# A gated two-layer cross-attention model on one core: rope's repeated query block removed, its halves exchanged by 64-partition vector instructions, a head pair's first projection one slot further ahead

## The reference, cut to what matters

```python
# x (8,112,512), ctx (8,375,128); 16 heads, K=128, D_CQ=384, R=64; layer 0's attention:
q_hk  = (layernorm(x) @ Wq.T).reshape(8, 112, 16, 128)
q_big = einsum('bshk,hkq->bshq', q_hk, w_kc_q)             # 384 wide
q_big = q_big*cos + rotate_half(q_big)*sin                 # rotate_half(x) = [-x[192:], x[:192]]
kv_r  = ctx*cos + rotate_half(ctx)*sin
q_r, k_r = q_big @ W_qr, kv_r @ W_kr                       # 64 wide
ctx_c = softmax(q_r @ k_r.T) @ kv_r                        # 112 x 375 scores per head
x = x + tanh(g) * ((ctx_c @ w_kc_kv.T) @ Wo.T)
# then a quantised feed-forward, a second attention (no rope on the query), a second feed-forward
```

## Time and profile before

| | |
|---|---|
| runs | 1081.9, 1082.13, 1083.32 us; median 1082.13 us |
| profiled execution | 1087.78 us, its span 1085.7 us, mean granted clock 0.983 |
| PE busy | 988.6 us, 91% of the span |
| DVE, ACT, POOL busy | 674.6, 530.9, 516.5 us |
| layer 0's attention | the first scores at 69.22 us, one pair of heads every 49.95 us |

### The profile page before, as it was taken

The page is one execution under the profiler, slowest core; times in us unless marked ns, Lnnn a source line. Parts: engine busy times, 40 slices in busy tenths (PEclk is TensorE's granted clock), DMA queues, the critical chain, the costliest instruction groups (busy, mean ns, idle before and its releaser), DMA issues. The chain is left out here.

```text
span 1085.7 us, 19735 instructions
## 1 busy us (share of the span) xinstructions
PE 988.6 (91%) x6228; PEld 575.3 (53%) x6237; DVE 674.6 (62%) x1176; ACT 530.9 (49%) x1238; POOL 516.5 (48%) x651
## 2 busy tenths in 40 slices
PE   0678999999999999899999689999999989999998
PEld 0335555555555555544444357777777754444543
DVE  2768787877878787659767726666666662423012
ACT  1245556565656566600257337777777772105400
POOL 1947666676666667511224326666666660200000
PEclk9999999999999999999999979999999999998999
DMA  8020312212130201055020122210222004104001
GB/s 216 25 81 19 102 48 64 68 43 68 43 92 29 92 19 30 11 198 191 1 69 30 40 68 69 69 34 34 68 68 68 1 1 184 39 1 165 1 29 39
DMA packets 24603, 68.24 MB, mean 63 GB/s; under 512 B 3696, under 2 KB 5872, under 8 KB 22259
## 3 DMA queue, kind: packets, MB, share of 16 engines
q1 hardware_dynamic: 18368, 56.70, 15.7%
q10 hardware_dynamic: 6192, 10.97, 3.8%
HBM read 63.98 MB, written 3.68 MB: 62 GB/s over the span
## 5 line engine op out<-in xcount | busy, mean ns | idle before, releaser
L1077 POOL TENSOR_SCALAR scratch<-scratch,rinv 112x375 f32<-112x375 f32 x256 | 155.4, 621 | 148.5 <-DVE rinv L944 148.5
L819 ACT ACTIVATE scratch<-ps,mxn 112x375 f32<-112x375 f32 x256 | 144.1, 571 | 58.5 <-DVE mxn L939 58.4
L939 DVE TENSOR_REDUCE mxn<-ps 112x2 f32<-112x750 f32 x128 | 119.5, 934 | 41.3 <-PE ps L633 41.3
L1059 POOL TENSOR_TENSOR scratch<-scratch 128x896 f32<-128x896 f32 x64 | 104.4, 1632 | 59.4 <-DVE scratch L963 58.9
L684 PE MATMUL ps<-xnT,scratch 128*128 128x448 f16 x576 | 125.1, 364 | 3.8 <-DVE scratch L1014 2.4
L671 PE MATMUL ps<-scratch,kvn_hi 125*128 125x224 f16 x768 | 119.9, 260 | 4.4 <-DVE scratch L985 2.3
L656 PEld LDWEIGHTS ps<-ident,scratch 112*125 112x125 f32 x768 | 100.0, 188 | 42.4 <-issue 35.3
L1069 POOL TENSOR_TENSOR scratch<-scratch 128x375 f16<-128x375 f32 x128 | 115.3, 901 | 10.9
L656 PE MATMUL ps<-ident,scratch 112*125 112x112 f32 x768 | 106.5, 275 | 10.9 <-DVE scratch L1005 9.1
L829 ACT ACTIVATE scratch<-ps 125x672 f16<-125x672 f32 x128 | 94.2, 736 | 43.5 <-PE ps L656 42.5
L963 DVE TENSOR_TENSOR scratch<-ps,ropeq 128x448 f32<-128x448 f32 x192 | 108.2, 615 | 7.3 <-PE ps L684 6.8
(11 more groups left out here) (161 smaller groups left out, 1485.6 us busy)
## 6 DMA issues: line engine op xcount, KB each, us to landing
scratch<-in_wq SPq DMA_DIRECT2D x16, 512.0 KB, 5.2
scratch<-in_wo SPq DMA_DIRECT2D x16, 512.0 KB, 3.7
wabs<-in_w ACTq DMA_DIRECT2D x32, 256.0 KB, 3.0
scratch<-in_w SPq DMA_DIRECT2D x8, 1024.0 KB, 4.9
scratch<-in_W SPq DMA_DIRECT2D x8, 1024.0 KB, 5.8
scratch<-in_kcq SPq DMA_DIRECT2D x8, 512.0 KB, 5.2
scratch<-in_qr SPq DMA_DIRECT2D x32, 128.0 KB, 3.1
scratch<-in_kcq SPq DMA_DIRECT2D x8, 384.0 KB, 3.2
```

The costliest lines, as they stand in the source:

```text
L819: last = nc.scalar.activation(prob[0:S, s % 2, hh, :], scores_ps[0:S, hh, 0:L], ACT.Exp, bias=mxn[0:S, s % 2, hh:hh + 1], accum_out=rsum[0 ...
L939: nc.vector.tensor_reduce(mxn[0:S, s % 2, :], scores_ps[0:S, :, 0:L], AX_X, ALU.max, negate=True).then_inc(max_done, 1)
L1059: nc.gpsimd.tensor_tensor(roped[:, u % 2, rows], roped[:, u % 2, rows], turned[:, rows], ALU.add).then_inc(rope_add, 1)
L1077: last = nc.gpsimd.tensor_scalar(prob[0:S, s % 2, hh, :], prob[0:S, s % 2, hh, :], rinv[0:S, s % 2, hh:hh + 1], P_SCALE, ALU.mult, ALU.mult)
```

## The change

Block 3 goes. Its table row in `ropeq` is loaded with its halves exchanged, and `rope` makes the rotated product of block 2 with two instructions of 64 partitions: one reads partitions 64 to 127 of PSUM and writes partitions 0 to 63, the other the reverse. `w_kc_q` is split for 384 channels per head, not 512. The blocks come in the order 2, 0, 1, and POOL's two additions count on semaphores of their own. The order on all engines is a new one: B comes early in a slot and A at its end; A 0 of the next pair stands in slot 3 ahead of C 1 (it was in slot 4), A 2 in slot 7 ahead of C 0 (it was in slot 0 of its own pair). SP loads Wq, w_kc_q, W_qr and W_kr one pair further ahead.

```diff
 TENSOR = ([
-    [TURN, SCORES, ("A", 2), ("S", 0), ("K", 2), *ropes(2, 0, 1)],
-    [TURN, SCORES, ("A", 3), ("S", 1), ("K", 3), *ropes(2, 2, 3)],
+    [TURN, SCORES, *ropes(2, 2, 0), ("S", 0), ("K", 2), ("A", 3)],
+    [TURN, SCORES, *ropes(2, 1), ("S", 1), ("K", 3), *ropes(3, 2)],
...
 VECTOR = ([
-    [SCORES, TURN, NORM, ("A", 3), ("S", 1), *ropes(2, 2, 3)],
+    [SCORES, TURN, *ropes(2, 1), NORM, ("S", 1), *ropes(3, 2)],
...
-            act.dma_start(ropeq[:, :, :], tab["ropeq"]).then_inc(s_ropeq, 16)
+            act.dma_start(ropeq[:, 0:5, :], tab["ropeq"][:, 0:5, :]).then_inc(s_ropeq, 16)
+            act.dma_start(ropeq[0:R, 5, :], tab["ropeq"][R:P, 5, :]).then_inc(s_ropeq, 16)
+            act.dma_start(ropeq[R:P, 5, :], tab["ropeq"][0:R, 5, :]).then_inc(s_ropeq, 16)
...
+            mixed = order[at["A", 0]:N_THIS] if layer == 0 else []
...
+                    def iteration(p):
+                        last = isinstance(p, int) and p + 2 >= PAIRS
+                        if is_batch(p) and is_batch(p + 1):
+                            weights(p + 1, "kckv", "wo")
+                        if not last:
+                            weights(p + 2, "wq", "kcq")
+                        if not last:
+                            weights(p + 2, "qr")
...
-                            pe.wait_ge(rope_add, nth(q, 8, 4 * n + 3))
+                            pe.wait_ge(rope_add, nth(q, 4, 2 * n + 1))
+                            pe.wait_ge(last_add, nth(q, 4, 2 * n + 1))
...
-                                       ((roped[:, u % 2, 2], 2),),
-                                       ((turned[:, 2], 5),))[j]:
+                                ((roped[:, u % 2, 2], 2, every, every), (turned[:, 2], 5, high, low),
+                                 (turned[:, 2], 5, low, high)))[j]:
+                            n_rows = rows.stop - rows.start
                             last = nc.vector.tensor_tensor(
-                                dst.rearrange("p (b n) -> p b n", b=B // 2), src,
-                                ropeq[:, t:t + 1, :].to_broadcast([P, B // 2, S]), ALU.mult)
+                                dst[to].rearrange("p (b n) -> p b n", b=B // 2), src[rows],
+                                ropeq[rows, t:t + 1, :].to_broadcast([n_rows, B // 2, S]),
+                                ALU.mult)
```

More of the change, by code:

```diff
@@ L260, in flamingo, with load_pair @@
         s_gate = sem("gates_done")
-        def load_pair(sp, layer, q, free=None):
+        def load_pair(sp, layer, q, free=None, names=()):
             order = ("qr", "kcq", "wq") if layer == 1 or free is not None else ("wq", "kcq", "qr")
-            for n in order + ("kckv", "wo"):
+            for n in names or order + ("kckv", "wo"):
                 src = w[f"{n}{layer}"][ds(q, 1)]
@@ L481, in attention @@
             N_THIS = at["C" if layer == 0 else "Q", 1] + 1
-            this = order[:N_THIS]
+            this = [g for g in order[:N_THIS] if g != ("A", 0)]
+            mixed = order[at["A", 0]:N_THIS] if layer == 0 else []
+            N_AHEAD = N_THIS - len(mixed)
             last_u = max((("U", 0), ("U", 1)), key=lambda g: (g in this, at[g]))
@@ L536, in first, with counts @@
                 return isinstance(p, int) and p < 0
+            def counts(p, g):
+                return 1 + any(x != g and g in mixed and not runs(p, x) for x in mixed)
             kv_behind = {5: (0, 1), 6: (2, 3, 4), 7: (5, 6, 7)}
@@ L616, in free @@
                                            nth_group(q - 1, ("M" if n == "wq" else "W", 0)))
-                        load_pair(sp, layer, q, free)
+                        load_pair(sp, layer, q, free, names)
+                    def iteration(p):
[6 more added lines that the diff above has]
+                            weights(p + 2, "qr")
+                    if layer == 0:
+                        iteration(-1)
+                        with sp.Fori(0, PAIRS - 2) as p:
+                            iteration(p)
+                        iteration(PAIRS - 2)
+                        iteration(PAIRS - 1)
+                    else:
+                        with sp.Fori(1, PAIRS) as q:
+                            weights(q)
                 @block.tensor
@@ L775, in group @@
                                         start=True, stop=True)
-                        last.then_inc(group_done, 1)
+                        last.then_inc(group_done, counts(p, g))
                     def iteration(p, slots=range(B)):
@@ L926, in _ @@
                     act.sem_inc(exp_done, 1)
-                    act.sem_inc(group_high, sum(g in split_order for g in this))
+                    act.sem_inc(group_high, sum(g in split_order for g in order[:N_AHEAD]))
                     iteration(-1)
```

105 lines of the change are left out of this document (56 added, 49 removed).

## The result

The changed kernel takes 1094.91 us (median of 4 runs, 1092.71 to 1096.45) where before takes 1082.02 beside it (4 runs): the ratio is 1.0119, with an interval of [1.0094, 1.0145]. It is slower by 12.9 us. The forecast was 1088, slower, with a range of 1076 to 1093: the direction holds, the size doesn't, and the median lies 1.9 us outside the range.

What follows compares the result with a forecast made beforehand. PE was taken as the bound, its gain nearly all given back as waits for DVE. Seven pairs +2.45, start +5.3, last pair -1.2: +6.5 us, 1087.78 to 1094.3; less 5.65, 1088.6, given as 1088, range 1076 to 1093.

Steps and rivals of the forecast that it cites:

- the places named: PE waits for DVE at A 3, A 1, U 0, A 0, X, R, B 1 2 and U 1: together 4.6 us a pair.
- the price of crossing: DVE instructions of block 2 that change partitions take 0.61 us, not 0.53: 1.0 us a pair on DVE, 0.85 on the path.
- the upper of the two bounds: A crossing DVE instruction can't start under the tail of the one before: 0.64 us; the lower bound was 0.53.
- the forecast's 0.85 a pair for the holds alone: Crossing price on the path: A 3 and A 1 0.17 each, U 0 0.26, B 1 2 / U 1 0.26.
- L 0 1.87 to its end: On DVE ahead of A 0 in slot 3, L 0 takes 1.87 us, giving PE a wait of 0.95.
- the 0.2 without a name: 0.2 us a pair added to the 4.6 of waits, for the unnamed part of PE's 2.95 us of waits in before.
- +5.3: Start of layer 0's attention: first scores later by 4.9 us, plus 0.4 with the price of crossing.
- the only stage that the change touches: Layer 0's attention alone was taken to be touched; the sum has no term for any other stage.
- It stood 5.65 over the median of the runs shown; taking that off: Before's profiled 1087.78 us stood 5.65 over the median 1082.13; subtracting this turned 1094.3 into 1088.6.
- All of the gain: Rival: the new waits don't arise and PE alone bounds, 29 us less, 1053; chance 0.03.
- crossing costs nothing: Rival: block 2's crossing on DVE is free; pairs -3.5, start +4.9, last pair -1.4, so 1082; chance 0.26.
- Slower still: Rival: crossing instructions take 0.64 and every wait is 0.1 longer, +0.5 us a pair more: 1092; no chance of its own.

Runs made afterwards that it cites:

- the straight halves: Changed kernel, but each of the two 64-partition instructions writes the half that it reads, so the exchange is left out: 1085.01 us, ratio 0.9983 to before.
- the changed kernel's second profile: Profiled execution of the changed kernel run again with no edit: 1094.53 us; median of that run 1094.24 us, ratio 1.0074 to before.

## Why the prediction was right or wrong

**Right: what bounds and the sign.** The gain of the matmuls was given back as waits for DVE, at the places named. Counted from start to start as in the prediction (forecast, with the price of crossing, in brackets): A 3 0.48 and A 1 0.41 (0.47 each), U 0 1.06 (1.16), R 0.72 (1.0), U 1 with the B 1 2 before it 0.89 (0.76), X of slots 0 and 4 0.46 (0.65). The pair is 50.49, forecast 50.3; that it came within 0.2 is luck, as the third point shows.

**Right: the crossing price.** 1.91 a block, forecast 1.84, against 1.59 if free; three steps of 0.64, the upper of the two bounds and not the 0.61 that was taken. The cause is the start partition differing from the last instruction's, not the crossing as such (the straight halves, 1.81). On the path, with L 0 standing still in none of the three: 48.81 with the halves crossed, 48.59 with them straight, 46.50 with one instruction. So crossing instead of writing straight costs 0.2 us a pair, and the third instruction together with its holds 2.1; no run tells those two apart, and the forecast's 0.85 a pair for the holds alone stays untested.

**Wrong: the price of L 0, "L 0 1.87 to its end".** The row of 1.87 was itself already an instruction that had stood still: alone 128x1024 takes 1.2 us, at this place 2.95. It was taken as a constant, though what POOL did at that moment was in the trace and the edit moved both. POOL in the kernel before, beside the L 0 at 242.45 of the earlier trace rows:

```profile
242.34 0.90 POOL L1069 TENSOR_TENSOR scratch<-scratch 128x375 f16<-128x375 f32 x1
243.22 2.13 POOL L1077 TENSOR_SCALAR scratch<-scratch,rinv 112x375 f32<-112x375 f32 x2
```

L 0 ended at 244.32, 1.08 after the first of them, as it ends 1.07 after the addition now; and the normalisation behind was long, 2.13, there too. PE's wait ahead of A 0 was 1.75 and not 0.95. The kernel with L 0 moved shows the full worth: 1.68 us a pair and 11 us of the whole (1094.2 and 1094.9 in two measurements against 1083.75). In the pair the error was hidden by others of the opposite sign: with L 0 undisturbed the pair is 48.8, and the forecast with 1.2 for L 0 would have been 49.6, 0.8 too long. The other waits were overstated by 0.5 together, R and X most, and of the 0.2 without a name hardly anything was there. X of slot 4 waits 0.14 and not 0.4: L 1 ahead of its half, put at three quarters of 1.6, takes 0.95, with no instruction of POOL beside it.

The Trainium skill states what was not weighed: by "SBUF — State Buffer", section "🔬 SBUF: two separate sides", a VectorE instruction with two SBUF inputs and a GpSimd instruction that reads SBUF take the same ports, one of them for its whole length while the other stands still. Here 2.95 is the rest of POOL's addition plus 1.07, and when L 0 goes first the addition is 2.99, 3.05 or 3.36 instead of 2.08: the traces agree with that. By the same section of the Trainium skill the one that starts first has the ports; by the records the addition started first by 0.20 and won, and by 0.22 and lost, so the profile's starts don't decide it at that distance.

**Wrong: the start, "+5.3".** This is the step that made most of the miss: the start is 8.2 us later in the first pair of profiles and 9.5 in the second (77.17 against 67.72). The walk took A 0 and A 1 at the lengths that they had in before (3.93 and, in the earlier trace rows, 2.43), but the change takes U 0 away from in front of A 0, and PE stands idle 4.1, 2.7 and 1.3 us. A 1 then ran with a granted clock of 0.50, 1.2 of 2.4 GHz, as the window shows:

```profile
54.00:57.50 3.50, 3.50 (x11) 1.43 (x10) 0.33 (x1) 0.00 (x0) 0.36 (x1) 0.50 0.00 0
```

That is 2.2 us in A 1, and with the 0.7 of A 0 (4.64 against 3.93) it makes the 2.9 that the forecast lacked. A 0 took nearly twice the 2.43 of a fast one, though its windows show no lower clock; with PE at work ahead of it, it took 2.43, and the scores came 1.6 earlier. The lengths don't settle the cause: in the kernel with L 0 moved A 1 takes 4.66 too, in a window with a clock of 1.00, and in the changed kernel's second profile A 0 and A 1 take 3.90 and 3.73, two blocks ahead of A 1 take 2.40 instead of 1.31, and the first scores come as late. The length of A 0 varies in before as well (2.43 and 3.93), which is 1.5 us of its start.

**Wrong: that the attention of layer 0 is "the only stage that the change touches".** Layer 1 is 1.0 us longer (the last section), and the sum puts it at nothing.

**"It stood 5.65 over the median of the runs shown; taking that off": fair, and the sum under it too small.** Profile to profile the forecast looks good, 1094.3 against 1095.87, and the changed kernel's profiled runs stand only 0.96 and 0.29 over their medians; so 4.7 of the 6.9 us between 1088 and 1094.91 seem to come from this step, 1.6 from the sum and 0.6 from rounding down. But the stretches that the change doesn't touch, between the stages of attention and behind layer 1's, took 375.0 us in the profile of before and 373.6 in that of the changed kernel, 375.5 and 371.6 in the second two, and 369.7 to 377.0 over all fourteen profiles. They are 371.5 in the middle, so 3.5 of the 5.65 lay there, and 1.5 more in the slow A 0: chance of that execution as far as two profiles of before tell, and fair to take off. Without these stretches the changed kernel is 9.4 us longer in the first pair of profiles and 11.7 in the second, beside 12.9 and 9.6 between medians. The forecast of that was 6.5. What was missing is 3 to 4 us of the start and the 1.0 of layer 1. That the two whole profiles differ by 8.0, near 6.5, is luck.

The range was too narrow as well. The 80 runs of before taken with the experiments go from 1080.6 to 1088.3 us: 42 have a clock of 0.986 or more and a median of 1082.85, 31 have 0.984 or less and a median of 1086.4. The changed kernel had 0.980 to 0.987 over nine runs, and seven of them 0.984 or less.

**The rivals.** "All of the gain" and "crossing costs nothing" are excluded by the rows above. "Slower still", 1092, came nearest in time, and has the step right (0.64), but not the waits, "every wait 0.1 longer": the one for L 0 apart, they came out 0.5 us shorter together than walked.

**Open.** Why the changed kernel's executions have the lower clock more often is seen in part: from 40 to 65 us its two profiles show a mean clock of 0.86, before's two 1.00, and 25 us at 0.86 take 0.003 off the mean of the whole. But the kernel with L 0 moved shows 1.00 there and has 0.980 to 0.984 in eight of ten runs, so that is not all of it. Nor is it settled how much of the distance between 12.9 and 9.6 us, two measurements of the same change, is chance.

## What to carry to other kernels

Before an instruction's length is used at a new place, look at what the engine that shares its memory ports did during the row it comes from: here 1.2, 1.87 and 2.95 us are one and the same instruction. Work taken from the engine that is busiest gives nothing while a second engine, busy 42 of 50 us, is on the path at seven places a pair; the same instructions gained 1.3% once the order gave PE other work at those places, so the order is to be walked on both engines before an edit is judged. And before two profiled executions are set against each other, compare the stretches that the change doesn't touch: here they differed by 1.4 and 3.9 us, and hid that much of the cost.

## What was not expected of the hardware

L 0 against POOL's addition: 0.20 us ahead, the addition costs L 0 1.75 us; 0.22 ahead, it is made to wait itself by 1.28. An entry moved by 0.3 us was worth 1.68 us a pair and some 11 us of 1095.

In layer 1, which the change doesn't touch, a pair takes 31.98 to 32.00 us in the changed kernel and in every kernel with three instructions for block 2 (seven kernels), and 31.87 in before and in every kernel with two or with block 3. The 0.12 lies in slot 7, at the turn of the loop (4.19 from one X to the next against 4.06), and the second pair takes 32.23: 1.0 us in all. What does it was not looked into.
